# Group statistics of the next image from a second read of it, spread over the even attention steps

## The reference, cut to what matters

```python
# layer 0: self-attention over 1024 pixels, 8 heads of 64
x = x + _L0_conv_ref(_gn(x), Wqkv, bqkv, Wout, bout)
# layer 1: deformable attention in 16 windows of 8x8, with offsets, sampling and an MLP for the bias
x = x + _L1_conv_ref(_gn(x), ...)

def _gn(v, G=32, eps=1e-5):          # 32 groups of 16 channels
    g = v.reshape(B_, G, C_ // G, H_, W_)
    m = jnp.mean(g, axis=(2, 3, 4), keepdims=True)
    s = jnp.var(g, axis=(2, 3, 4), keepdims=True)
    return ((g - m) / jnp.sqrt(s + eps)).reshape(v.shape)
```

## Time and profile before

| what | value |
|---|---|
| median of 3 runs | 3209.77 us (3202.72 to 3211.99) |
| the profiled execution's own time | 3210.39 us |
| its span, first to last instruction | 3208.6 us |
| mean granted TensorE clock | 0.969 |
| PE busy | 3000.6 us, 94% of the span |
| DVE busy | 2205.4 us, 69% |
| ACT busy | 1656.9 us, 52% |

### The profile page before, as it was taken

How to read it: one execution, slowest core, us unless ns; L and a number is a source line. 1 busy time by engine, 2 the same in 40 slices (tenths; PEclk the granted TensorE clock), 3 DMA queues, 4 the chain that set the end, 5 groups by cost and what they waited for, 6 DMA issues and landing times.

```text
span 3208.6 us, 51471 instructions
## 1 busy us (share of the span) xinstructions
PE 3000.6 (94%) x20600; PEld 2107.4 (66%) x20600; DVE 2205.4 (69%) x2934; ACT 1656.9 (52%) x2429; POOL 196.1 (6%) x157
## 2 busy tenths in 40 slices
PE   6999799999999999999999999999999999998958
PEld 5777577756776577665776657775677756775434
DVE  5666566586675876757767677677776686665846
ACT  2553465374553655536555456546465374553624
POOL 0000020000200002000020000200020000200200
PEclk9999899999999999999999999999999999998968
DMA  5223013311124011240113310232112311104040
GB/s 189 56 51 105 27 30 87 106 62 50 35 76 140 26 52 36 75 163 7 53 36 95 135 40 23 62 115 87 41 30 88 106 62 50 35 12 163 1 114 27
DMA packets 141502, 220.58 MB, mean 69 GB/s; under 512 B 77713, under 2 KB 96660, under 8 KB 137396
## 3 DMA queue, kind: packets, MB, share of 16 engines
q1 hardware_dynamic: 136596, 190.03, 18.7%
q10 hardware_dynamic: 4672, 27.26, 2.7%
HBM read 162.40 MB, written 54.84 MB: 68 GB/s over the span
## 4 chain that ended last, share of the span: by engine, by line
PE 80%; DVE 9%; DMA 4%; ACT 2%; issue 2%; SPq 2%; DVEq 0%; POOL 0%; ACTq 0%
PE banks L658 14%; PE banks L671 13%; PE banks L642 12%; PE banks L613 11%; PE banks L603 5%; PE banks L850 4%; PE banks L713 4%; PE banks L860 3%; PE banks L851 3%; PE banks L852 3%; DMA point_outputs_dram<-point_outputs 3%; PE banks L823 2%; SPq L474 2%; DVE qk_halves L1565 1%; DVE neg_max L1387 1%
## 5 line engine op out<-in xcount | busy, mean ns | idle before, releaser
L1387 DVE TENSOR_REDUCE neg_max<-banks 128x1 f32<-128x1024 f32 x512 | 602.1, 1218 | 97.9 <-PE banks L642 97.2
L1077 ACT ACTIVATE exps_turned<-banks 128x1024 f32<-128x1024 f32 x256 | 262.7, 1026 | 714.4 <-PE banks L658 714.4
L1396 DVE COPY exps_turned<-banks 128x1024 f32<-128x1024 f32 x256 | 313.5, 1225 | 425.0 <-PE banks L658 422.0
L1067 ACT ACTIVATE exps<-banks,neg_max 128x1024 f32<-128x1024 f32 x512 | 565.6, 1114 | 42.1 <-DVE neg_max L1387 41.8
L658 PE MATMUL banks<-ident,exps 128*128 128x128 f32 x4096 | 559.3, 280 | 15.4 <-DVE exps_turned L1396 14.6
L658 PEld LDWEIGHTS banks<-ident,exps 128*128 128x128 f32 x4096 | 455.0, 142 | 174.5 <-issue 135.7
L642 PE MATMUL banks<-qk_halves 64*128 64x512 f32 x3072 | 439.8, 419 | 53.3 <-ACT exps L1067 39.6
L671 PE MATMUL banks<-exps_turned,values 128*64 128x256 f32 x4096 | 479.1, 383 | 0.8 <-issue 0.8
L671 PEld LDWEIGHTS banks<-exps_turned,values 128*64 128x64 f32 x4096 | 279.6, 137 | 153.5 <-issue 30.4
L642 PEld LDWEIGHTS banks<-qk_halves 64*128 64x128 f32 x3072 | 287.3, 190 | 138.2 <-issue 98.5
L1565 DVE SCALAR_TENSOR_TENSOR qk_halves<-banks,qk_halves 128x1024 fp32r<-128x1024 f32 x256 | 301.8, 1219 | 88.9 <-ACT qk_halves L1116 88.7
(11 more groups left out here) (181 smaller groups left out, 3337.6 us busy)
## 6 DMA issues: line engine op xcount, KB each, us to landing
wqk_ring<-wqk_split SPq DMA_DIRECT2D x62, 512.0 KB, 4.2
wo_halves<-wo_split_dram SPq DMA_DIRECT2D x8, 2048.0 KB, 7.5
exps_turned<-in_x SPq DMA_DIRECT2D x32, 512.0 KB, 5.3
x_dram<-exps SPq DMA_DIRECT2D x32, 512.0 KB, 2.6
exps_turned<-x_dram SPq DMA_DIRECT2D x32, 512.0 KB, 6.3
out<-exps_turned SPq DMA_DIRECT2D x32, 512.0 KB, 2.7
recips_b<-recips_dram SPq DMA_DIRECT2D x240, 64.0 KB, 3.7
x_image<-in_x ACTq DMA_DIRECT2D x14, 1024.0 KB, 10.3
```

The lines of the kernel that those rows point to most:

```text
L1067: freed(act.activation(PB[:, 2 * h + n % 2], slot(("s", m, i)), ACT.Exp, bias=NM[:, m:m + 1], accum_out=SS[:, m:m + 1]), ("s", m, i))
L1387: dve.tensor_reduce(NM[:, m:m + 1], slot(("s", m, i)), AX.X, ALU.max, negate=True).then_inc(mx, 1)
L1396: dve.tensor_copy(PT[:, n // 2 % 2, 1, :, P * j:P * j + P], TB.rearrange("p s (k q) -> p (s k) q", k=4)).then_inc(t_free[1], 1)
```

## The change

ACT asks for a second, earlier copy of the next image, in eight blocks of 128 channels x 512 columns (256 KB each, one 2 KB row per partition), into two buffers that it takes in turn: XSAMPLE[0] is the space of the convolution's sums and gelu, XSAMPLE[1] that of the probabilities. Blocks 0 and 1 are asked for at the end of ACT's step 5, blocks 2 to 7 at the end of its steps 7, 9, 11, 13, 15 and 17. DVE takes `bn_stats` of block c in step 6 + 2c, directly behind `row_max` and ahead of `hats`, `log_row` and `copy_turned` of that step. The joining to channels moves to step 21, `group_sums` and `group_variance` to step 22 (the matmul now writes columns 0 to 7 of MB, which PE's `turn_weights` of step 23 waits for), `normalise` to steps 25 and 26, `x_high` to steps 26 and 27, and `x_low` to one in each of steps 27 to 30, all ahead of `copy_turned`. The full load of X in step 22 stays as it is.

```diff
+            def load_sample(c, k):
+                wait_after(act, xs_done, 8 * (k - 1) + c - 1)
+                if c == 1:
+                    wait_after(act, o1_full, 2 * (k - 2))
+                act.dma_start(XSAMPLE[c % 2][:], x[k, P * (c // 2):P * (c // 2) + P, 512 * (c % 2):512 * (c % 2) + 512])\
+                    .then_inc(xs_in[c % 2], 16)
...
-                    if i + 1 < B and n in (27, 28):
-                        x_high(2 * (n - 27), i + 1)
-                        x_high(2 * (n - 27) + 1, i + 1)
+                    if i + 1 < B and n in (26, 27):
+                        x_high(2 * (n - 26), i + 1)
+                        x_high(2 * (n - 26) + 1, i + 1)
...
+                    if i + 1 < B and n == 5:
+                        load_sample(0, i + 1)
+                        load_sample(1, i + 1)
+                    if i + 1 < B and n in range(7, 19, 2):
+                        load_sample((n - 3) // 2, i + 1)
...
+            def sample_stats(c, k):
+                dve.wait_ge(xs_in[c % 2], 64 * (k - 1) + 16 * (c // 2 + 1))
+                dve.bn_stats(BNS[:, c // 2, c % 2], XSAMPLE[c % 2][:]).then_inc(xs_done, 1)
...
                     if i + 1 < B:
-                        if n == 24:
+                        if n in range(6, 22, 2):
+                            sample_stats((n - 6) // 2, i + 1)
+                        if n == 21:
+                            dve.wait_ge(xs_done, 8 * (i + 1))
+                            channel_means()
+                        if n == 25:
                             dve.wait_ge(x_in[0], 16 * (i + 1))
-                            group_parts(X, 0)
-                            group_parts(X, 1)
-                        if n == 25:
-                            dve.wait_ge(x_in[1], 16 * (i + 1))
-                            group_parts(X, 2)
-                        if n == 26:
-                            group_channels(group_parts(X, 3))
-                        if n == 27:
                             dve.wait_ge(gn_rstd, 2 * i + 2)
                             normalise(0)
                             normalise(1)
-                        if n == 28:
+                        if n == 26:
+                            dve.wait_ge(x_in[1], 16 * (i + 1))
                             normalise(2)
                             normalise(3)
-                        if n == 29:
-                            x_low(1, i + 1)
-                        if n == 30:
-                            x_low(3, i + 1)
+                        if 27 <= n < 31:
+                            x_low(n - 27, i + 1)
...
-                    if i + 1 < B and n == 26:
-                        group_variance(2 * i + 2, GSO)
+                    if i + 1 < B and n == 22:
+                        group_variance(2 * i + 2, GSM)
```

More of the change, by code:

```diff
@@ L183, in build @@
         RB = sb("recips_b", [P, 2, 256])
-        T4 = sb("conv_sums", [P, 256])
-        TG = sb("conv_gelu", [P, CT, 64])
+        CVS = sb("conv_or_sample", [P, 512])
+        T4 = CVS[:, 0:256]
+        TG = CVS[:, 256:512].rearrange("p (t c) -> p t c", t=CT)
         OFF = sb("offsets", [64, 16])
@@ L196, in build @@
         SM = sb("sim", [P, PXT * CT, 8])
-        SMP = sb("probabilities", [P, 2, 4, 32])
-        AT2 = sb("probabilities_turned", [P, 4, 64])
+        SMB = sb("probs_or_sample", [P, 512])
+        SMP = SMB[:, 0:256].rearrange("p (h l e) -> p h l e", h=2, l=4)
+        AT2 = SMB[:, 256:512].rearrange("p (c n) -> p c n", c=4)
+        XSAMPLE = (CVS, SMB)
         SMX = sb("sim_max", [P, 64])
@@ L207, in build @@
         MB = PS[:, 7]
-        GSO = MB[:, 256:264]
         GSM = MB[:, 0:8]
@@ L243, in build @@
         wqk_raw = sem("wqk_raw_in")
+        xs_in = [sem("x_sample_in0"), sem("x_sample_in1")]
+        xs_done = sem("x_sample_done")
         gn_in = sem("gn_in")
@@ L731, in turn_weights @@
                     pe.wait_ge(piece_free, (j + 2) * MAXES)
+                if j + 2 < B:
+                    pe.wait_ge(gn_var, 2 * j + 4)
                 for t in range(CT):
@@ L764, in similarities @@
                 pe.wait_ge(kz_done, j + 1)
-                if f == 0 and j + 2 < B:
-                    pe.wait_ge(gn_var, 2 * j + 4)
                 wait_after(pe, sim_done, 2 * j + f)
@@ L974, in _ @@
                         sampled_keys(i - 1)
-                    if i + 1 < B and n == 26:
-                        group_sums(2 * i + 2, GSO)
+                    if i + 1 < B and n == 22:
+                        pe.wait_ge(piece_free, (i + 1) * MAXES)
+                        group_sums(2 * i + 2, GSM)
                     if i and n == 27:
@@ L1081, in gelu @@
                 act.wait_ge(conv_done, j + 1)
-                act.activation(TG[:].rearrange("p t c -> p (t c)"), T4[:], ACT.Gelu, bias=CB[:, 0:1])\
+                act.activation(TG.rearrange("p t c -> p (t c)"), T4, ACT.Gelu, bias=CB[:, 0:1])\
                     .then_inc(gelu_done, 1)
@@ L1156, in keep_probabilities @@
                 act.wait_ge(probs_full, j + 1)
-                act.activation(AT2[:].rearrange("p c n -> p (c n)"), OB[:, 0:256], ACT.Copy).then_inc(probs_kept, 1)
+                act.activation(AT2.rearrange("p c n -> p (c n)"), OB[:, 0:256], ACT.Copy).then_inc(probs_kept, 1)
             def wo_high():
@@ L1334, in group_parts, with channel_means @@
                 return ins
+            def sample_stats(c, k):
+                dve.wait_ge(xs_in[c % 2], 64 * (k - 1) + 16 * (c // 2 + 1))
+                dve.bn_stats(BNS[:, c // 2, c % 2], XSAMPLE[c % 2][:]).then_inc(xs_done, 1)
             def group_channels(last):
                 link(last)
+                channel_means()
+            def channel_means():
                 dve.memset(PAUSE[:], 0.0)
@@ L1470, in convolve_sum @@
                 dve.wait_ge(dve_step, after)
-                ins = dve.tensor_reduce(T4[:].rearrange("p (u o) -> p u o", o=4)[:, :, n],
+                ins = dve.tensor_reduce(T4.rearrange("p (u o) -> p u o", o=4)[:, :, n],
                                         PROD.rearrange("p (u e) -> p u e", e=25), AX.X, ALU.add)
@@ L1670, in _ @@
                         sampled(1, i - 1)
-                    if i + 1 < B and n == 28:
-                        x_low(0, i + 1)
                     if i and n == 28:
@@ L1681, in _ @@
                     if i + 1 < B:
-                        if n == 24:
-                            dve.wait_ge(x_in[0], 16 * (i + 1))
-                            group_parts(X, 0)
-                            group_parts(X, 1)
-                        if n == 25:
-                            dve.wait_ge(x_in[1], 16 * (i + 1))
-                            group_parts(X, 2)
-                        if n == 26:
-                            group_channels(group_parts(X, 3))
-                        if n == 27:
+                        if n in range(6, 22, 2):
+                            sample_stats((n - 6) // 2, i + 1)
+                        if n == 21:
+                            dve.wait_ge(xs_done, 8 * (i + 1))
+                            channel_means()
+                        if n == 25:
+                            dve.wait_ge(x_in[0], 16 * (i + 1))
                             dve.wait_ge(gn_rstd, 2 * i + 2)
@@ L1720, in _ @@
                     copy_turned(n, i)
-                    if i + 1 < B and n == 26:
-                        group_variance(2 * i + 2, GSO)
+                    if i + 1 < B and n == 22:
+                        group_variance(2 * i + 2, GSM)
                     if i and n == 26:
                         key_blocks(i - 1)
-                    if i + 1 < B and n == 29:
-                        x_low(2, i + 1)
                     if n == 0:
```

## The result

The changed kernel takes 3228.97 us (median of 4 runs, 3228.38 to 3233.72) against 3207.42 (median of 4, 3202.72 to 3211.99) of the kernel before in the same comparison: ratio 1.0071 [1.0052, 1.0089], 0.7% slower. The forecast was 3243, slower, with 3200 to 3257 as the range. The profiled execution took 3228.38 us, with a span of 3226.6, 18.0 longer than before.

What follows compares the result with a forecast made beforehand. PE, busy for 94% of the span, was taken as the bound. Losses of 33.6 + 2.5 + 9.6 less 12.5 won gave +33.2 us on 3210.39, and with the median 0.6 lower 3243 us; range 3200 to 3257.

Steps and rivals of the forecast that it cites:

- block 0 is late: Step 6: block 0 lands late, DVE's copy_turned(6) is held up, and PE waits 5.6 us in images 1 to 6.
- The other seven `bn_stats`: Steps 8 to 20: blocks 1 to 7 are asked for early enough that DVE has no idle time before their statistics.
- PE's waits of step 7: Ahead of step 7's transposes PE waits for copy_turned, 5.6 us in each of images 1 to 6, 33.6 us.
- the clock's part: PE's lower granted clock behind its wait of step 7: 1.6 us in each of six images, 9.6 in all.
- image 0: PE's wait in image 0, which has neither log nor hats: 2.5 us lost.
- L: Time from block 0's issue to its landing, taken as 9 us, range 3.7 to 11.3, from ACT's slow next-image loads.
- rival A: Block 0 lands like SP's loads, in 3.7 to 4.2 us; time 3199 to 3202 us; chance 0.20.
- The last ten steps: Moving statistics out of steps 24 to 26 shortens PE's waits by 2.0 us per image: 12.5 us won in all.
- 23 us in all: The most that can be won: PE's waits, 3.8 us in each of six images and 0.5 in image 0.

Runs made afterwards that it cites:

- e1: The changed kernel with its two sample buffers swapped and block 0 asked for at the end of step 1: 3189.02 us, ratio 0.9937 to the kernel before.
- e2: The changed kernel with the bn_stats of block 0 taken in step 7 behind copy_turned, request unmoved: 3187.91 us, ratio 0.9933 to the kernel before.
- e3: The changed kernel with block 0 asked for at the end of step 4, one step earlier: 3185.14 us, ratio 0.9925 to the kernel before.
- e7: e3 with x_low number 2 behind copy_turned of step 29, as in the kernel before: 3188.62 us, ratio 0.9928 to the kernel before.
- e4: The changed kernel with SP's reciprocals written as 128 rows of 16 bytes, outputs scaled wrongly: 3184.46 us, ratio 0.9921 to the kernel before.
- e9: e3 and e8 together, block 0 asked for in step 4 and 8 byte elements: 3184.74 us, ratio 0.9925 to the kernel before.
- e6: The kernel before without the eight bn_stats of steps 24 to 26, images normalised with wrong numbers: 3190.35 us, ratio 0.9934 to the kernel before.
- e8: The changed kernel with SP's reciprocals written as 256 elements of 8 bytes, computation complete: 3181.22 us, ratio 0.9909 to the kernel before.

## Why the prediction came out as it did

*Direction and mechanism.* Right: block 0 is late, blocks `copy_turned(6)`, and PE pays. e1, e2 and e3 show it by three different ways to remove the wait. The other seven `bn_stats` have no idle time for a DMA before them, as forecast.

*The size of the loss.* The terms gave 33.6 + 2.5 + 9.6 = 45.7 us; the anchors show 46.4, and the change against e3 43.8. Part of this agreement is luck, since the terms were off in both directions: PE's waits of step 7 came to 29.9 us where 33.6 was forecast, image 0 to 0.7 where 2.5 was, what remains beyond all waits, the clock's part, to 12.6 where 9.6 was, and 3.2 us are waits in images 4 to 6 that the forecast didn't have. L was taken as 9 from an issue at 1578.4 behind `log`. Measured it is 10.65 us (10.4 to 11.0 in images 1 to 6), but the request goes out 2.3 us before `log` has ended, since here ACT's request ran ahead of its computing (1579.70, with `log` ending at 1581.96): 10.65 - 2.3 - 3.4 = 5.0, against 5.6 forecast and 5.00 measured. The clock costs more than forecast: 4 us at 0.50 to 0.52 is 2.0 in image 4 where rows 13 gave 1.6; in images 1 to 4 and 6 it is 1.6 to 2.5, by what each lost beyond its waits. In image 0 block 0 took 8.2 us, not 9, and was asked for 1.1 us sooner than supposed (108.12, 0.07 us ahead of a write), which gives the 0.7. In image 5 there is one more PE wait, of 2.2 us, with a dip behind it. I didn't trace its cause; e7, in which block 0 isn't late, has one of 2.7 us in the same image, so it doesn't belong to the late block.

*The reason for L.* Wrong. I took the slow start for a property of the long unused queue or of an unread image. It is the shadow of SP's write of 512 single elements, which was in the trace of the kernel before, at the same moments as the slow loads. In all seven images `next_image` was asked for 3.8 us behind such a write, and that write's read back followed 8.7 to 11.4 us behind the write (in image 4 write 1682.46, load 1686.27, read back 1693.84), so that "all are slow" said nothing about the queue. The number was right because block 0 falls into the same shadow; a request one step earlier doesn't, and I would have forecast the same L for it. The rival A, with 3.7 to 4.2 us, had the price of an undisturbed load nearly right: 3.2 to 5.4 us in e3, 3.9 to 5.6 in e4.

*The undisturbed load.* In e3 the load of image 4 took 3.2 us without a write of reciprocals beside it, and in e9 2.6 to 2.8. The Trainium skill ("DMA: Bandwidth & Descriptors", anatomy of one DMA) leads to the estimate of 2.6 us, by a fit that it gives for DMAs issued from GpSimd: near the undisturbed load, and four times too short for the one in the shadow. The same page of the Trainium skill (Specifications) asks for at least 512 bytes for full rate; both SP's 4 byte elements and the 16 byte rows of e4 are below that, and the runs show 10.1 us for the one and 1.55 for the other.

*The last ten steps.* The term that was mis-sized: 12.5 us forecast, 23.0 measured. The waits went as worked out: 3.8 us per image became 1.9 (1.8 forecast), with 0.56 in step 25, 0.23 behind step 26 and 1.09 in step 29. In the stretch from `next_image` to the values, between the two anchors, PE's idle time fell by 2.1 us in image 4, and its busy time by 0.6, which I can't assign. The step that failed is the sentence that set the most that can be won at 3.8 us per image, "23 us in all": it counted the waits and not the clock behind them. In four images of six the wait for the statistics was followed by the dip that e6 removes, 1.7 us each by its rows and 1.5 by the anchors, some 6 of the 10.5 us that the term lacked; the 0.6 to 0.8 us per image that I can't assign are most of the rest. I looked for dips behind long idle times only, and this wait has 1.07 us. The measured 23.0 meets that bound by accident.

*What is left.* The stretches between the images, in which nothing was changed, took 8.2 us less. PE's work there is the same and dips of the clock lie in other places: before, the stretch from 1814 to 1820 has 0.68, 0.50 and 0.97, and the kernel after has no dip there; behind image 4 PE's busy time is 2.7 us less, and the stretch 2.8 us shorter. Why a dip comes in one trace and not in the other, no run here separates. Without these 8.2 us the span would have been 3234.8. The forecast's 3243 was 14 us above the median: 10.5 from the last ten steps, 8.2 from the stretches between, less 2.8 at the end and 0.7 in the loss makes 15 by the traces.

## What to carry to other kernels

Before you give a slow DMA a property of its queue, look at what other queues have in flight at that moment, and above all for writes of single elements; try the load once beside them and once away from them. When work is moved off a critical path into a full stretch, ask for its operand so early that it is there even with the slowest landing that the trace shows: one step made the difference of 44 us here. Count a short wait of PE with the clock that may follow it.

## What the runs showed of the hardware

- A write of 512 elements of 4 bytes, 2 KB in all, takes 9.2 us (median of 120 in the change) until its read back is asked for, 256 elements of 8 bytes 3.6 (e8), 128 rows of 16 bytes 1.4 (e4). A load of 256 KB on ACT's queue that is asked for 1.8 us behind the first kind takes 10.4 to 11.0 us (images 1 to 6 of the change), against 3.2 to 5.4 with none on its way (e3). What inside the DMA engines holds it, and whether the number or the size of the elements counts, no run shows.
- ACT's DMA request was issued at 1579.70 while an ACTIVATE that began at 1579.54 ran and `log` had not begun: there the request didn't stand behind the computing ahead of it in the program.
- A PE wait of 1.07 us was followed by some 4 us at a granted clock of 0.50 to 0.79 in four images, which cost 1.5 us each, and by no fall of the clock in two (the kernel before).
